# Splitting the experts' first weight on GpSimd in the first two batches, with the low halves kept in memory until the transition

## What is computed

```python
u = x @ W_in + b_in                                  # 256 -> 768
uc = short_conv(u, short_w, short_b)                 # 3 taps over the tokens
x0, x1, v = split(uc, 3)
v = causal_fft_conv(v * x1, gen_filter(...), filter_bias)
x = layernorm(x + (v * x0) @ W_out + b_out)

probs = softmax(x @ gate_w.T)                        # 16 experts, the best 4 of each token
top_w, top_idx = top_k(probs, 4); top_w = top_w / top_w.sum()
h = silu(x @ w1[e].T) * (x @ w3[e].T)                # 128 hidden values
moe = sum over the 4 experts of top_w * (h @ w2[e].T)
shared = silu(x @ sw1.T) * (x @ sw3.T) @ sw2.T
x = layernorm(x + moe + shared)
```

## Time and profile before

| | us |
|---|---|
| median of three runs | 626.38 (626.25 to 626.77) |
| the profiled execution | 617.06 |
| its span, first to last instruction | 615.2 |
| TensorE busy, matmuls | 527.1 |
| VectorE busy | 449.4 |
| ScalarE busy | 370.5 |
| GpSimd busy | 347.3 |
| mean granted clock of TensorE, full is 1 | 0.935 |
| phase 1 ends, first expert product starts | 327.4 |

### The profile page before, as it was taken

How to read it: one execution, slowest core, us unless ns; L and a number is a source line. 1 busy time by engine, 2 the same in 40 slices (tenths; PEclk the granted TensorE clock), 3 DMA queues, 4 the chain that set the end, 5 groups by cost and what they waited for, 6 DMA issues and landing times.

```text
span 615.2 us, 11085 instructions
## 1 busy us (share of the span) xinstructions
PE 527.1 (86%) x3184; PEld 456.8 (74%) x3184; DVE 449.4 (73%) x1053; ACT 370.5 (60%) x844; POOL 347.3 (56%) x320
## 2 busy tenths in 40 slices
PE   5997999999999989598387789898988989899762
PEld 2786878787877778476257679897978989888651
DVE  5878899999898999678597724444445778877544
ACT  4745486868685867534272436565756566776444
POOL 0332124868686886628738655555555667667630
PEclk9997999999999999987858799899999998999778
DMA  7999553988594748429935865555548999889964
GB/s 241 198 234 329 71 126 113 280 225 200 113 228 141 192 146 184 142 62 314 350 98 182 235 184 156 164 157 152 181 149 283 297 300 307 286 289 320 337 218 142
DMA packets 79006, 128.07 MB, mean 208 GB/s; under 512 B 10358, under 2 KB 57911, under 8 KB 78650
## 3 DMA queue, kind: packets, MB, share of 16 engines
q1 hardware_dynamic: 42714, 61.21, 34.9%
q0 software_dynamic: 28688, 58.35, 33.8%
q10 hardware_dynamic: 7552, 7.88, 3.6%
HBM read 75.89 MB, written 47.35 MB: 200 GB/s over the span
## 4 chain that ended last, share of the span: by engine, by line
PE 53%; DVE 20%; ACT 9%; issue 8%; another core or an unknown queue 4%; DMA 3%; SPq 2%; POOL 1%; ACTq 0%; DVEq 0%; POOLq 0%
PE bank L1034 7%; PE bank L1036 7%; PE bank L817 7%; PE bank L1035 7%; PE bank L839 5%; PE bank L871 4%; PE bank L1085 4%; PE bank L953 2%; PE bank L1057 2%; PE bank L1003 2%; PE bank L991 2%; SPq L541 1%; DVE w_lo L1610 1%; ACT ty L1318 1%
## 5 line engine op out<-in xcount | busy, mean ns | idle before, releaser
L784 POOL DMA_INDIRECT token_parts<-ty,goes x144 | 142.4, 989 | 91.4 <-issue 32.7
L755 POOL DMA_INDIRECT expert_rows<-row,slot x112 | 128.7, 1150 | 74.4 <-issue 32.0
L1034 PE MATMUL bank<-w_hi,xtT_hi 128*128 x288 | 89.9, 312 | 10.2 <-DVE xtT_lo L1783 7.7
L1035 PE MATMUL bank<-w_lo,xtT_hi 128*128 x288 | 84.2, 292 | 0.4 <-issue 0.4
L1036 PE MATMUL bank<-w_hi,xtT_lo 128*128 x288 | 83.1, 288 | 1.5 <-issue 1.5
L1034 PEld LDWEIGHTS bank<-w_hi,xtT_hi 128*128 128x128 f32 x288 | 57.1, 198 | 14.5 <-issue 14.3
L1783 DVE TENSOR_TENSOR xtT_lo<-bank,xtT_hi 128x512 fp32r<-128x512 f32 x72 | 49.5, 689 | 20.6 <-issue 14.2
L1768 DVE TENSOR_TENSOR taT_lo<-bank,taT_hi 128x256 fp32r<-128x256 f32 x72 | 30.3, 421 | 44.8 <-ACT taT_hi L1290 26.4
L1296 ACT ACTIVATE tsl<-bank 128x256 f32<-128x256 f32 x72 | 29.6, 411 | 55.0 <-PE bank L1036 29.5
L1318 ACT ACTIVATE ty<-bank,tail 128x256 f32<-128x256 f32 x144 | 62.0, 494 | 0.0
L1035 PEld LDWEIGHTS bank<-w_lo,xtT_hi 128*128 128x128 f32 x288 | 57.2, 199 | 1.8 <-issue 1.8
(11 more groups left out here) (212 smaller groups left out, 1356.2 us busy)
## 6 DMA issues: line engine op xcount, KB each, us to landing
xt<-expert_rows SPq DMA_DIRECT2D x144, 129.0 KB
row<-token_parts SPq DMA_DIRECT2D x18, 640.0 KB
xT<-in_xT SPq DMA_DIRECT2D x8, 512.0 KB
xtok<-in_b_out SPq DMA_DIRECT2D x8, 512.0 KB
xtok<-in_x POOLq DMA_DIRECT2D x8, 512.0 KB
x<-taps POOLq DMA_DIRECT2D x8, 512.0 KB
x<-ups POOLq DMA_DIRECT2D x8, 512.0 KB
w_hi<-in_w POOLq DMA_DIRECT2D x1, 4096.0 KB, 16.9
```

The source lines that it names most:

```text
L755: pool.indirect_dma_start(out=rows_d, out_offset=bass.IndirectOffsetOnAxis(ap=slot[q][:, n:n + 1], axis=0), in_=src[:, n // TOPK, n % TOPK ...
L784: pool.indirect_dma_start(out=parts_d, out_offset=bass.IndirectOffsetOnAxis(ap=goes[:, q_ * UNROLL + u:q_ * UNROLL + u + 1].bitcast(U32), ...
L1034: te_.matmul(ps, x_hi, w_hi, start=first, stop=False)
L1035: te_.matmul(ps, x_hi, w_lo, start=False, stop=False)
```

## The change

The first weight's low halves are made in batches 0 and 1. Eight raw pieces of 128x1024 (512 KB each) go through the buffer `row`, cut into four places: SyncE loads a piece from w13 (`load_raw`), GpSimd subtracts w13_hi in place (`rest_w`), and SyncE stores the result to a new array in memory, `w13_rest` (`store_rest`). The second four loads wait until their place's store has landed. `load_w13` reads its four parts from w13_rest instead of w13, at the same places of SyncE's program. The eight `low13` on VectorE are gone, and TensorE waits ahead of the first product for the four loads. ld_moe is split into two semaphores. fill_rows(0) and end_rows(0, ...) wait until all pieces are stored.

```diff
+        rest_d = nc.dram_tensor("w13_rest", [P, W13], F32, kind="Internal").ap()
+        raw = [early[:, n * LOW:(n + 1) * LOW] for n in range(RAW)]          # RAW = 4
@@ SyncE
             def load_w13(n):
-                k = E // NPART
-                sp.dma_start(w13_lo[:, n * PART:(n + 1) * PART].bitcast(F32).rearrange("p (e c n) -> p e c n", e=k, c=DC),
-                             io["w13"][n * k:(n + 1) * k].rearrange("e (c p) n -> p e c n", p=P)).then_inc(ld_w13[n], 16)
+                for s in range(RAW):
+                    sp.wait_ge(rest_out[s], 16 * (W13 // LOW // RAW))
+                sp.dma_start(w13_lo[:, n * PART:(n + 1) * PART].bitcast(F32), rest_d[:, n * PART:(n + 1) * PART]).then_inc(ld_w13[n], 16)
+            def load_raw(n):
+                s, k = n % RAW, LOW // (DC * 2 * HID)
+                if n < RAW:
+                    sp.wait_ge(k_filt, 2)
+                else:
+                    sp.wait_ge(rest_out[s], 16 * (n // RAW))
+                sp.dma_start(raw[s].rearrange("p (e c n) -> p e c n", e=k, c=DC),
+                             io["w13"][n * k:(n + 1) * k].rearrange("e (c p) n -> p e c n", p=P)).then_inc(ld_raw[s], 16)
+            def store_rest(n):
+                sp.wait_ge(rest_made, n + 1)
+                sp.dma_start(rest_d[:, n * LOW:(n + 1) * LOW], raw[n % RAW]).then_inc(rest_out[n % RAW], 16)
             def body(i, q, h):
+                if is0(i):
+                    for n in range(RAW):
+                        load_raw(n)
                 if two_next(i):
                     load_xT(i + 2)
+                if is0(i):
+                    for n in range(2):
+                        store_rest(n)
+                        load_raw(n + RAW)
+                if is1(i):
+                    for n in range(RAW, 2 * RAW):
+                        store_rest(n)
...
                     sp.wait_ge(dve_r, 2 * (i + 1))
                     sp.dma_start(xtok[:, :, :], bias).then_inc(ld_bias, 16)
+                if is0(i):
+                    for n in range(2, RAW):
+                        store_rest(n)
+                        load_raw(n + RAW)
@@ GpSimd
+            def rest_w(n):
+                s, at = n % RAW, slice(n * LOW, (n + 1) * LOW)
+                pool.wait_ge(ld_moe, 16)
+                pool.wait_ge(ld_raw[s], 16 * (n // RAW + 1))
+                nc.gpsimd.tensor_tensor(out=raw[s].bitcast(F32R), in0=raw[s], in1=w13_hi[:, at].bitcast(F32),
+                                        op=ALU.subtract).then_inc(rest_made, 1)
                 if is1(i):
                     add_x(i)
+                    for n in range(4, 6):
+                        rest_w(n)
                 if two_next(i):
                     round_x(i + 2)
+                if is0(i) or is1(i):
+                    for n in (range(6, 8) if is1(i) else range(2)):
+                        rest_w(n)
...
                 if has_next(i) and is0(i):
                     add_newest(i + 1, 1 - q)
+                    for n in range(2, 4):
+                        rest_w(n)
@@ TensorE, ahead of the first product
-                        pe_e.wait_ge(lo_made, W13 // LOW)
+                        for n in range(NPART):
+                            pe_e.wait_ge(ld_w13[n], 16)
@@ ScalarE, fill_rows, and VectorE, end_rows
+                if is0(i):
+                    for s in range(RAW):
+                        act.wait_ge(rest_out[s], 16 * (W13 // LOW // RAW))
@@ VectorE
-                    for n in range(3):
-                        low13(n)
                     dve.wait_ge(cut_made, len(CUTS))
                     table(0)
...
                     logits(i, 4)
-                    low13(3)
                     top(i)
                     add_shared(i - 1, 1 - q, h - 1 if q == 0 else h)
-                    low13(4)
                     slots(i, q, h, 5)
...
-                    for n in range(5, W13 // LOW):
-                        low13(n)
```

More of the change, by code:

```diff
@@ L79 @@
 LOW = 1024
+RAW = 4
 GROUPS = (range(8), range(8, TT * TOPK))
@@ L336, in build @@
         ld_w13 = [sem(f"ld_w13_{n}") for n in range(NPART)]
-        ld_w2, lo_made = sem("ld_w2"), sem("lo_made")
+        ld_w2, lo_made, ld_moe2, rest_made = (sem(n) for n in ("ld_w2", "lo_made", "ld_moe2", "rest_made"))
+        ld_raw = [sem(f"ld_raw{n}") for n in range(RAW)]
+        rest_out = [sem(f"rest_out{n}") for n in range(RAW)]
         res_out = [sem(f"res_out{u}") for u in range(UNROLL)]
@@ L703, in body @@
                     pool.dma_start(w2_hi[:, :].rearrange("p (e d) -> p e d", e=E),
-                                   io["w2"].rearrange("e h d -> h e d")).then_inc(ld_moe, 16)
+                                   io["w2"].rearrange("e h d -> h e d")).then_inc(ld_moe2, 16)
                 third = not (is0(i) or is1(i))
@@ L1023, in _ @@
             batches(pe_e, body)
-            pe_e.wait_ge(ld_moe, 32)
+            pe_e.wait_ge(ld_moe, 16)
+            pe_e.wait_ge(ld_moe2, 16)
             pe_e.wait_ge(tab_ready, 32)
@@ L1093, in turn @@
                         pe_e.wait_ge(dve_acc, 2 * B)
-                        pe_e.wait_ge(lo_made, (W13 + W2) // LOW)
+                        pe_e.wait_ge(lo_made, W2 // LOW)
                     pe_e.wait_ge(t_alo, k + 1)
@@ L1572, in body @@
                     norm_scales(i)
-                    dve.wait_ge(ld_moe, 32)
-                    for n in range(3):
-                        low13(n)
+                    dve.wait_ge(ld_moe2, 16)
                     dve.wait_ge(cut_made, len(CUTS))
@@ L1603, in body @@
                     end_rows(i - 1, 0)
-            def low13(n):
-                if n % (PART // LOW) == 0:
-                    dve.wait_ge(ld_w13[n // (PART // LOW)], 16)
-                at = slice(n * LOW, (n + 1) * LOW)
-                ve.tensor_tensor(w13_lo[:, at], w13_lo[:, at].bitcast(F32), w13_hi[:, at].bitcast(F32),
-                                 ALU.subtract).then_inc(lo_made, 1)
             def low2(n):
@@ L1705, in end_rows @@
                 at = slice(half * TT // 2, (half + 1) * TT // 2)
+                if is0(i):
+                    for s in range(RAW):
+                        dve.wait_ge(rest_out[s], 16 * (W13 // LOW // RAW))
                 if row_of(i) is row:
```

## The result

| | before | after |
|---|---|---|
| median of the runs | 626.32 us (6 runs, 614.63 to 628.17) | 638.66 us (6 runs, 628.29 to 641.92) |
| profiled execution | 617.06 us, span 615.2 us | 637.62 us, span 635.8 us |
| mean granted clock | 0.935 | 0.934 |

The ratio is 1.0246, with a 95% interval from 1.0159 to 1.0332: the changed kernel is slower, by some 15 us (10 to 21) by this ratio and by 12.3 us by the two medians. Every ratio in this document leaves out the slow executions, those more than 1.5% above the quickest of their kernel, so it need not be the quotient of the medians, which are of all executions. The two spans lie 20.6 us apart, because the profiled execution of before was one of its quick ones.

A forecast was written before the change was run, and what follows sets the result against it. VectorE's convolutions, products and z were taken to bound the early batches. Holds 5.4 + 10.8, clock 2.3, transition -3.4 make +15.1 us: 632.2 for the profiled execution, plus 9.3 to the median, 641.5 us; range 630 to 649.

The forecast's parts named there:

- Pieces 0 and 1: Batch 0: start when w13_hi lands at 53.4, beside VectorE lines 1434 and 1441, making z 5.4 us late.
- Pieces 2 and 3: After add_newest(1), at about 70 us: beside VectorE lines 1696 and 1452, which are not held, 0 us.
- Pieces 4 to 7: After add_x(1) and round_x(3): beside VectorE's two-operand lines 1514 to 1538 and 1434, all held, 10.8 us.
- The clock: TensorE's lines 861 and 871 run slower after longer idling, 0 to 2.0 + 2.6 us; half taken, 2.3.
- The transition: Last batch to expert tiles: without three VectorE subtractions after slots(8), the first product comes 3.4 us earlier.
- It leaves with table(0): Transition: the xt load leaves with a table that three subtractions held up, so it comes 3.5 us earlier.
- SyncE's chain: Early batches: last store lands at about 94, fill_rows(0) needs it at 97.26; 3 us of cover, no cost.
- Rival (C): SyncE's store, wait, load chain slips, last raw pieces and fill_rows(0) late: 3 to 8 us more, 647; chance 0.08.
- The sum: Whole kernel: 5.4 + 10.8 + 2.3 - 3.4 = +15.1 us on the span of 615.2 us.
- Rival (A): Early batches: VectorE's back-to-back instructions keep GpSimd out until a one-operand instruction or hole; +7.4 us, 633.8; chance 0.21.
- Rival (B): At most one piece paid in full, only the transition counts: 621.5 to 625.7 us, middle 623.0; chance 0.13.
- Rival (D): Transition: the low half's load from memory is late and TensorE waits for it; no size given, chance 0.02.

The follow-up runs named there:

- subs_alone: Kernel before plus eight GpSimd subtractions at the change's places, results unused, loads, stores and transition unchanged: 571.99 us against 561.72, ratio 1.0209.
- write_only: Changed kernel with each GpSimd subtraction replaced by a fill with zeros, loads and stores kept: 562.74 us against 561.72 of the kernel before, ratio 1.0012.
- the two placements: Kernel before plus two GpSimd subtractions, beside VectorE's last convolution group of batch 0 or in its gap: ratios 1.0040 and 0.9978.
- no_raw_loads: Changed kernel with zero fills instead of subtractions and without the eight raw loads: 558.44 us against 562.78 of the kernel before, ratio 0.9944.
- two_beside: Kernel before plus two GpSimd subtractions beside VectorE's last convolution group of batch 0: 565.81 us against 562.78, ratio 1.0040.
- no_low: Kernel before without VectorE's eight low-half subtractions, the raw weight standing for the low half: 559.36 us, ratio 0.9956.
- two_in_gap: Kernel before plus two GpSimd subtractions in batch 0's gap, where VectorE reads banks or idles: 561.91 us against 562.78, ratio 0.9978.
- the repeated run: Changed kernel unaltered, measured again beside the kernel before on one chip: 574.57 us against 562.78, ratio 1.0203.

## Why the prediction was right, point by point

The forecast was 641.5 us in a range of 630 to 649, slower with 0.87; 638.66 was measured. The mechanism was the one named, GpSimd's subtraction holds VectorE's two-operand instructions, and subs_alone, write_only and the two placements show it, each from another side. The terms of the sum fared unequally, and that the total came out so close is in part luck, as the first two terms show. Batch 2's first transform was forecast near 114 us and started at 111.77.

- **Pieces 0 and 1, 5.4 us: measured 0.** The prediction named the condition, w13_hi landing after 57 us. It landed at 56.56, just inside that bound, but VectorE was by then in its last pair of instructions with two SBUF operands of the batch. The step that failed is the landing time: I had costed only the 2 MB ahead on the DMA (2.65 us). The transfer itself took 1.5 us longer (18.4 instead of 16.9), but the load was issued 4.2 us later, at 38.13 instead of 33.91, because GpSimd's add in front of it waited 5.90 us for a transfer (1.69 before). The raw loads did that: without them the wait was 1.88 and 1.95 us (no_raw_loads, subs_alone), with them and without subtractions 6.87 (write_only). Where w13_hi landed at 51 us (subs_alone, two_beside), the pair made the group 3.3 us longer, for 4.3 and 4.6 us of GpSimd's time.
- **Pieces 2 and 3, 0: measured 5.42.** The same error seen from the other side. I had placed them beside lines 1696 and 1452 by a batch 0 that ends 5.4 us late. As it did not, VectorE was on to its products when they started at 68.87. In subs_alone, where the first pair did hold, they stood where I had placed them and cost 1.5 us (line 1489). The two errors cancel, 5.4 against 5.42, and that is luck.
- **Pieces 4 to 7, 10.8: measured 5.15 + 2.02 + 2.19 = 9.4.** The step holds. The price of one is a little under a whole piece (2.3 instead of 2.7), since pieces 6 and 7 waited for their raw loads and started a little before or after VectorE's own instruction.
- **The clock, 2.3: measured about 1.2.** Lines 910 and 920 took 1.98 + 5.61 in batch 1, 1.23 + 3.72 before (with the small overlap of the rows, +2.4), but in batch 0 they took 1.1 us less than before.
- **The transition, -3.4: measured -1.5 at the first product (-1.4 on the quick chips, 6.07 to 4.65), and -2.4 in the time when VectorE does no low half at all.** The failed step is "It leaves with table(0)", said of the xt load, and from it "so it comes 3.5 us earlier". The load also waits for the scatters and for the table's transfer. On the quick chips it came 1.5 us earlier in the changed kernel and not at all in no_low, and TensorE waited 1.50 us for its last rows: the subtraction had hidden that wait, so what the trace of before showed as a wait for VectorE was in part a wait for the tiles. On the first chip the load did come 3.1 us earlier and held nothing. There ScalarE's xtT_hi was late behind a gap without a named releaser, and whether such a gap belongs to the change stays open.
- **SyncE's chain, "3 us of cover", 0: measured 0 in the changed kernel, but for a reason other than mine.** The last store was to land at 94; it was issued at 95.8. Rival (C) was thus right about the chain, and GpSimd did wait at pieces 6 and 7 (1.41 and 2.29 us). It only did not show, because the holds gave the chain 15 us. In the kernels without holds it cost ScalarE 7.8 us of waiting, and 3.4 us in the time of write_only against no_low.
- **The sum.** Holds 14.8, clock 1.2 and transition -2.4 make +13.6, where I had +15.1. Measured are 12.3 us by the medians and some 15 (10 to 21) by the ratio, and 11.4 (8.7 to 14.2) on a quick chip, where single executions lie closer together. The noise of the first chip does not tell +13.6 from +15.1.
- **Rival (A)**, that VectorE's run keeps GpSimd out, is refuted by line 1569 at 68.59: its row starts 0.28 us before GpSimd's, and it is VectorE that waits, through both pieces. **Rival (B)** needed at most one piece paid in full; pieces 2 to 5 were, and 6 and 7 for 2.0 and 2.2 us. **Rival (D)** did not come: no wait for w13_lo's loads stands ahead of the first product in either trace of the changed kernel.

## What to carry to other kernels

- Work moved from VectorE to an idle GpSimd is free only where VectorE reads banks, has one SBUF operand, or waits. Lay GpSimd's new instructions over VectorE's timeline row by row; each one that falls on a run of two-operand instructions costs nearly its whole length, for as long as VectorE is on the path. Here eight pieces of 2.7 us cost 14.8 us, and two in a gap nothing.
- A wait in the trace gives an upper bound for what removing its cause brings. Look for the next thing that would be late (here the load of the tiles' rows) and list all that it waits for (here the scatters and the table's transfer beside the table). Shift it along with the gain only if all of these shift.
- When an experiment takes the suspected cost away and the time does not fall below the kernel before, though the change should gain, look for a second cost under the first. Without the holds the last store was late; only a run that removed both got to -3.1 us.

## What the runs showed of the hardware

- One waiting VectorE instruction stood through two GpSimd subtractions in a row (6.64 us instead of 1.22, and 5.83 instead of 0.68). It did not get in between them, although in other places it did: in subs_alone, lines 1537 and 1540 were held by one piece each, by 1.7 us. And line 1495's two instructions kept their 1.28 us in both traces of the changed kernel, though GpSimd's first pair started beside them (59.00 and 59.39 in the repeated run). That pair took 5.43 and 5.46 us, the longest of the pairs, so there it may have been GpSimd that waited; no row shows who goes first.
- GpSimd pays as well: 1.88 us for a piece while VectorE reads banks or idles, 2.32 beside VectorE (two_in_gap and two_beside); and writing alone takes less (1.2 us at the median for the same number of elements).
- Chips differ by more than this change: the kernel before took 562 us on three and 626 to 629 on two. On the latter the traces have gaps with no named releaser of up to 12 us, and single executions of one kernel lie 20 us apart (617.14 to 637.78). One kernel came out at 0.9968 on one chip and at 1.0164 on another, so a change worth a few us has to be measured on the chips it is for. What these gaps are was not found.
